# Block 1's inverse roots: one GpSimd power in place of a logarithm, an exponential and a correcting step, with new beats

## The reference, cut to what matters

```python
def _layernorm(x, axis=-1, eps=1e-05):
    m = jnp.mean(x, axis=axis, keepdims=True)
    v = jnp.var(x, axis=axis, keepdims=True)
    return (x - m) / jnp.sqrt(v + eps)
...
q = l2norm(q); k = l2norm(k)          # 16 heads of 64, each token's head by itself
dots = einsum('bhid,bhjd->bhij', q, k) * 10
dots = einsum('hg,bgij->bhij', W_pre_th, dots)      # "premix"
# causal mask; all but the 64 largest of a row are dropped; softmax
attn = einsum('hg,bgij->bhij', W_post_th, attn)     # "mix back"
out = einsum('bhij,bhjd->bhid', attn, v) * scale, times sigmoid(gates), @ Wo
x = _layernorm(x + out)
x = _layernorm(x + ffn(x))            # silu gate, two hidden layers with gelu
```

## Time and profile before

| | us |
|---|---|
| median of 3 runs | 3859.69 |
| lowest and highest run | 3850.48, 3867.26 |
| profiled execution | 3863.54 |
| its span (first to last instruction) | 3862.2 |
| TensorE busy | 3518.2 |
| VectorE busy | 3405.6 |
| ScalarE busy | 3078.7 |
| GpSimd busy | 1751.2 |
| granted TensorE clock, mean | 0.961 of full speed |

### The profile page before, as it was taken

How to read it: one execution, slowest core, us unless ns; L and a number is a source line. 1 busy time by engine, 2 the same in 40 slices (tenths; PEclk the granted TensorE clock), 3 DMA queues, 4 the chain that set the end, 5 groups by cost and what they waited for, 6 DMA issues and landing times.

```text
span 3862.2 us, 78954 instructions
## 1 busy us (share of the span) xinstructions
PE 3518.2 (91%) x19551; PEld 2607.6 (68%) x19551; DVE 3405.6 (88%) x18541; ACT 3078.7 (80%) x10773; POOL 1751.2 (45%) x3672
## 2 busy tenths in 40 slices
PE   4999999996799999999999999999999999999987
PEld 3888888873566666666666666666666666666665
DVE  6888888853999999999999999999999999999994
ACT  5777777755788888888888888888888888888864
POOL 0000000002556556565656555656666665665553
PEclk7999999996899999999999999999999999999999
DMA  3000000001111111111111111111111111111110
GB/s 125 12 12 9 12 12 12 10 6 35 26 28 28 29 32 28 28 32 34 33 30 28 28 29 28 28 28 30 31 28 29 34 33 33 28 28 29 26 26 4
DMA packets 168124, 106.01 MB, mean 27 GB/s; under 512 B 78000, under 2 KB 165104, under 8 KB 166896
## 3 DMA queue, kind: packets, MB, share of 16 engines
q1 hardware_dynamic: 167664, 100.96, 12.2%
HBM read 20.70 MB, written 8.91 MB: 8 GB/s over the span
## 4 chain that ended last, share of the span: by engine, by line
PE 32%; DVE 25%; ACT 16%; SPq 10%; DMA 8%; issue 7%; POOL 2%; DVEq 0%; ACTq 0%; POOLq 0%
SPq L1264 9%; DVE W L1736 8%; DMA T<-SN 8%; PE bank L362 6%; DVE last L1757 6%; ACT SN L1529 5%; PE bank L1336 4%; PE bank L1321 3%; PE bank L1413 3%; ACT T L1516 3%; PE bank L330 3%; PE bank L194 3%; PE bank L1348 2%; DVE y L895 2%; ACT L1485 2%
## 5 line engine op out<-in xcount | busy, mean ns | idle before, releaser
L1736 DVE MATCH_REPLACE8 W<-last,W 128x130 f32<-128x130 f32 (+17 forms) x3456 | 889.9, 269 | 0.0
L1757 DVE MAX8 last<-W 128x8 f32<-128x130 f32 (+17 forms) x3456 | 780.0, 271 | 0.0
L1842 POOL TENSOR_SCALAR posts<-post,share 128x128 f32<-128x128 f32 x1024 | 368.2, 378 | 372.7 <-DVE share L1666 372.7
L1336 PE MATMUL bank<-T,pre 128*128 128x40 f32 (+15 forms) x1024 | 402.8, 477 | 107.3 <-DMA T<-SN 79.1
L885 DVE TENSOR_TENSOR_SCAN hs<-dA,dx 128x256 f32<-128x256 f32 x512 | 353.2, 690 | 133.9 <-issue 100.5
L1516 ACT ACTIVATE T<-T,peak 128x260 f32<-128x260 f32 (+15 forms) x1024 | 416.7, 435 | 30.1 <-POOL T L1893 28.2
L1529 ACT ACTIVATE SN<-bank,rq 128x260 f32<-128x260 f32 (+1 forms) x1024 | 361.1, 433 | 88.0 <-DMA T<-SN 43.8
L1893 POOL TENSOR_TENSOR T<-T,below 128x520 f32<-128x520 f32 (+12 forms) x416 | 360.6, 883 | 23.1 <-DVE below L1766 7.6
L1336 PEld LDWEIGHTS bank<-T,pre 128*128 128x128 f32 x1024 | 173.4, 199 | 278.1 <-ACT T L1537 119.1
L1348 PEld LDWEIGHTS bank<-posts,T 128*128 128x128 f32 (+7 forms) x2048 | 267.9, 185 | 110.3 <-issue 54.7
L1348 PE MATMUL bank<-posts,T 128*128 128x128 f32 (+7 forms) x2048 | 324.4, 298 | 18.7 <-POOL posts L1842 17.2
(11 more groups left out here) (244 smaller groups left out, 9611.2 us busy)
## 6 DMA issues: line engine op xcount, KB each, us to landing
T<-SN SPq DMA_DIRECT2D x32, 130.0 KB
x_in<-in_xT SPq DMA_DIRECT2D x32, 128.0 KB, 2.2
x_mid<-x_b SPq DMA_DIRECT2D x32, 128.0 KB, 1.7
xb<-x_mid SPq DMA_DIRECT2D x32, 128.0 KB, 2.1
out_y<-x_d SPq DMA_DIRECT2D x32, 128.0 KB, 3.4
T<-SN SPq DMA_DIRECT2D x32, 126.0 KB
T<-SN SPq DMA_DIRECT2D x32, 122.0 KB
T<-SN SPq DMA_DIRECT2D x32, 118.0 KB
```

The costliest lines, as they stand in the source:

```text
L1336: pe.matmul(MIX[:, 0:pair.shape[-1]], pre[:], pair, start=True, stop=True).then_inc(premixed, 1)
L1736: dve.match_replace(both[:, s, at:to], best[n], both[:, s, at:to], LOWEST).then_inc(ranked, 1)
L1757: dve.max(best[n], both[:, s, at:to]).then_inc(ranked, 1)
L1842: pool.tensor_scalar(posts[(4 * k + j) % NP][:], post[:], share[k % 2][:, j:j + 1], 1.0, ALU.mult, ALU.mult).then_inc(posts_made, 1)
```

## The change

In the attention phase's two norms, for q and for k, `Root` is gone. GpSimd raises the clipped sums, or the variance with its epsilon, to the power -0.5 in one `tensor_tensor` with `ALU.pow` against a tile `power` that holds -0.5. ScalarE keeps in the norms only the copy with the epsilon (`act_lift`). Its table set for exponentials is now the one without the logarithm, and the gates' tanh no longer asks for the set of silu. The mixer phase's norms and the memory keys keep `Root`. New waits guard the tiles that the power writes or reads. All beat tables of the attention phase are new, and the loops run over one period more. Parts of the diff that only rename or repeat are left out.

```diff
@@ -36,7 +36,7 @@
-EXP_LN, SILU, GELU = "natural_log_exp_and_others", "silu_and_others", "gelu_and_others"
+EXP_LN, EXP, SILU, GELU = "natural_log_exp_and_others", "exp_and_others", "silu_and_others", "gelu_and_others"
@@ -96,12 +96,12 @@
     def __init__(self, room, sems, name, banks, sh, after, tiles):
...
-        self.var, self.rs, self.t = (room.sb(f"{name}_{n}", [P, 2]) for n in ("var", "rs", "t"))
-        self.meanmat, self.ident, self.eps = sh.meanmat, sh.ident, sh.eps
+        self.var, self.rs = (room.sb(f"{name}_{n}", [P, 2]) for n in ("var", "rs"))
+        self.meanmat, self.ident, self.eps, self.power = sh.meanmat, sh.ident, sh.eps, sh.power
...
-        self.lifted, self.normed, self.root = after.lifted, after.normed, after.root
+        self.lifted, self.normed, self.rooted = after.lifted, after.normed, sems.sem(name + "_rooted")
@@ -115,20 +115,20 @@
-    def act_root(self, act, k):
+    def act_lift(self, act, k):
...
-        act.wait_ge(self.lifted, k + 1)
-        self.root.act_guess(act, k, self.var[:], self.rs[:], self.t[:])
...
     def pool_root(self, pool, k):
-        k += self.base
-        self.root.pool_step(pool, k, self.var[:], self.rs[:], self.t[:])
+        pool.wait_ge(self.lifted, self.base + k + 1)
+        if k:
+            pool.wait_ge(self.spread, k)
+        pool.tensor_tensor(self.rs[:], self.var[:], self.power[:, 0:2], ALU.pow).then_inc(self.rooted, 1)
...
     def pe_spread(self, pe, k):
...
-        pe.wait_ge(self.root.stepped, Root.STEPS * (k + 1))
+        pe.wait_ge(self.rooted, k + 1 - self.base)
@@ -409,10 +409,10 @@
-        self.q_sq, self.q_t, self.rq = (room.sb(n, [P, 2 * HEADS]) for n in ("q_sq", "q_t", "rq"))
-        self.k_sq, self.k_t, self.rk = (room.sbs(n, [P, HEADS], 2) for n in ("k_sq", "k_t", "rk"))
+        self.q_sq, self.rq = (room.sb(n, [P, 2 * HEADS]) for n in ("q_sq", "rq"))
+        self.k_sq, self.rk = (room.sbs(n, [P, HEADS], 2) for n in ("k_sq", "rk"))
         self.x_loaded = sems.sems("xb_loaded", NXB)
-        self.q_root, self.k_root = Root(sems, "q"), Root(sems, "k")
+        self.q_rooted, self.k_rooted = sems.sem("q_rooted"), sems.sem("k_rooted")
@@ -480,12 +480,8 @@
-    def k_guess(self, act, b, t):
-        act.wait_ge(self.k_clipped, 2 * b + t + 1)
-        self.k_root.act_guess(act, 2 * b + t, self.k_sq[t][:], self.rk[t][:], self.k_t[t][:])
-
     def k_scale(self, act, b, t):
-        act.wait_ge(self.k_root.stepped, Root.STEPS * (2 * b + t + 1))
+        act.wait_ge(self.k_rooted, 2 * b + t + 1)
@@ -512,16 +508,15 @@
-    def q_guess(self, act, b):
-        act.wait_ge(self.q_clipped, b + 1)
-        self.q_root.act_guess(act, b, self.q_sq[:], self.rq[:], self.q_t[:])
-
     def k_clip(self, pool, b, t):
...
-    def k_step(self, pool, b, t):
-        self.k_root.pool_step(pool, 2 * b + t, self.k_sq[t][:], self.rk[t][:], self.k_t[t][:])
+    def k_power(self, pool, b, t):
+        pool.wait_ge(self.k_clipped, 2 * b + t + 1)
+        if b:
+            pool.wait_ge(self.k_scaled, 4 * (b - 1) + 2 * t + 2)
+        pool.tensor_tensor(self.rk[t][:], self.k_sq[t][:], self.sh.power[:, 0:HEADS], ALU.pow).then_inc(self.k_rooted, 1)
@@ -535,17 +530,22 @@
     def first_scale(self, dve, t):
-        dve.wait_ge(self.k_root.stepped, Root.STEPS * (t + 1))
+        dve.wait_ge(self.k_rooted, t + 1)
...
-    def q_step(self, pool, b):
-        self.q_root.pool_step(pool, b, self.q_sq[:], self.rq[:], self.q_t[:])
+    def q_power(self, pool, b):
+        pool.wait_ge(self.q_clipped, b + 1)
+        if b:
+            pool.wait_ge(self.s_kept, S_ALL * b)
+        pool.tensor_tensor(self.rq[:], self.q_sq[:], self.sh.power[:], ALU.pow).then_inc(self.q_rooted, 1)
...
     def q_clip(self, dve, b):
...
+        if b:
+            dve.wait_ge(self.q_rooted, b)
@@ -563,6 +563,7 @@
+        self.power, self.power_set = room.sb("power", [P, 2 * HEADS]), room.sem("power_set")
@@ -837,13 +838,11 @@
-                front.k_guess(act, 0, 0)
...
-                front.k_guess(act, 0, 1)
@@ -1031,11 +1029,13 @@
+        pool.memset(sh.power[:], -0.5).then_inc(sh.power_set, 1)
         mk_root.pool_step(pool, 0, mkv[:, 1:2], mkv[:, 3:4], mkv[:, 2:3])
+        pool.wait_ge(sh.power_set, 1)
...
-            front.k_step(pool, 0, t)
-        front.q_step(pool, 0)
+            front.k_power(pool, 0, t)
+        front.q_power(pool, 0)
@@ -1055,7 +1055,7 @@
-    SLOT, PERIODS = 16, SEQS + 2
+    SLOT, PERIODS = 16, SEQS + 3
@@ -1163,68 +1163,66 @@
-    PE_K = (-7, -6, 3, 3)
-    PE_K_TURN = (1, 2, 11, 24)
-    PE_Q = (11, 20, 23, 33)
-    PE_Q_SUM = (26, 30, 35, 36)
-    PE_Q_TURN = 44
-    PE_ATTEND = (5, 8, 8, 18)
-    PE_GATES = (34, 37, 39, 40)
-    PE_MIX = (56, 71, 89, 96, 121, 125, 126, 129)
-    PE_OUT = 25
-    PE_VAR1 = 33
-    PE_SPREAD1 = 38
-    PE_W1 = 41
-    PE_W2 = 45
-    PE_H1 = (63, 67, 67, 69)
-    PE_H2 = (79, 80, 91, 93)
-    PE_SCORE0 = (55, 60, 63)
-    PE_W3 = 94
-    PE_SCORE1 = (89, 91, 93, 95, 96, 100, 105, 107)
-    PE_VAR2 = 98
-    PE_SPREAD2 = 109
-    PE_V = (123, 127, 128, 128)
-    PE_PREMIX = [[71, 83, 89, 93, 104, 105, 118, 123], [125, 125, 128, 131, 136, 148, 164, 197]]
-    ACT_K = (-33, -24, 17, 21)
-    ACT_K_TURN = (9, 27, 30, 38)
-    ACT_Q = (30, 42, 43, 43)
-    ACT_K_ROOT = (-16, 24)
-    ACT_Q_SUM = 48
-    ACT_Q_ROOT = 55
-    ACT_PEAK = (-8, 33, 38, 42, 70, 78, 92, 114)
-    ACT_WIDE = (34, 39, 56, 69, 70, 80, 98, 123)
-    ACT_NARROW = (37, 41, 59, 69, 73, 85, 102, 127)
-    ACT_MIX = (68, 70, 72, 94, 96, 110, 119, 142)
-    ACT_SQUARE1 = 42
-    ACT_ROOT1 = 44
-    ACT_GATES = (44, 44, 51, 51)
-    ACT_SILU = (51, 52)
-    ACT_SCORE0 = (56, 63, 65)
-    ACT_H1 = (67, 68)
-    ACT_H2 = (74, 77)
-    ACT_SCORE1 = (72, 74, 77, 84, 85, 89, 91, 93)
-    ACT_SQUARE2 = 82
-    ACT_ROOT2 = 88
-    ACT_V = (114, 130, 138, 141)
-    ACT_PREMIX = [[69, 70, 75, 84, 90, 92, 97, 103], [109, 115, 144, 149, 158, 165, 191, 196]]
-    DVE_SHARE = (65, 83, 85, 98, 114, 117, 124, 136)
-    POOL_GATES = (15, 15, 17, 20)
-    POOL_OPEN = (80, 83, 85, 125)
-    ACT_CTX = (26, 28, 29, 33)
-    DVE_END1 = 62
-    DVE_Q_CLIP = 67
-    DVE_GATED = (73, 73)
-    DVE_END2 = 120
-    POOL_TURN = (-65, -65, -65, 8, 27, 56, 73, 63)
-    POOL_SHARE = (36, 62, 62, 80, 95, 106, 107, 124)
-    POOL_DROP = (8, 18, 34, 54, 67, 82, 105, 111)
-    POOL_ROOT1 = 25
-    POOL_Q_ROOT = 44
-    POOL_ROOT2 = 83
-    POOL_PREMIX = [[79, 80, 87, 104, 107, 107, 108, 110], [110, 122, 134, 139, 162, 168, 184, 193]]
-    ACT_K_SCALE = (3, 28)
-    POOL_K_CLIP = (-21, 10)
-    POOL_K_ROOT = (-14, 12)
+    PE_K = (1, 6, 21, 22)
+    PE_K_TURN = (18, 29, 34, 39)
+    PE_Q = (34, 36, 38, 44)
+    PE_Q_SUM = (42, 44, 48, 50)
+    PE_Q_TURN = 51
+    PE_ATTEND = (30, 31, 33, 34)
+    PE_GATES = (45, 51, 56, 60)
+    PE_MIX = (65, 79, 94, 106, 133, 136, 139, 146)
+    PE_OUT = 39
+    PE_VAR1 = 45
+    PE_SPREAD1 = 52
+    PE_W1 = 58
+    PE_W2 = 64
+    PE_H1 = (67, 72, 76, 78)
+    PE_H2 = (80, 89, 91, 95)
+    PE_SCORE0 = (64, 65, 69)
+    PE_W3 = 102
+    PE_SCORE1 = (85, 94, 96, 102, 103, 109, 115, 122)
+    PE_VAR2 = 112
+    PE_SPREAD2 = 136
+    PE_V = (141, 142, 145, 145)
+    PE_PREMIX = [[83, 91, 94, 102, 117, 123, 126, 135], [137, 140, 144, 156, 160, 165, 172, 204]]
+    ACT_K = (-38, -26, 1, 2)
+    ACT_K_TURN = (-5, 6, 20, 21)
+    ACT_Q = (18, 21, 23, 23)
+    ACT_Q_SUM = 33
+    ACT_PEAK = (-15, 5, 23, 36, 50, 58, 86, 109)
+    ACT_WIDE = (20, 22, 37, 44, 52, 74, 87, 111)
+    ACT_NARROW = (21, 33, 40, 47, 53, 80, 93, 111)
+    ACT_MIX = (46, 52, 70, 85, 91, 97, 106, 126)
+    ACT_SQUARE1 = 22
+    ACT_LIFT1 = 24
+    ACT_GATES = (23, 34, 38, 39)
+    ACT_SILU = (37, 37)
+    ACT_SCORE0 = (41, 43, 43)
+    ACT_H1 = (47, 50)
+    ACT_H2 = (53, 71)
+    ACT_SCORE1 = (55, 70, 73, 74, 78, 80, 82, 84)
+    ACT_SQUARE2 = 74
+    ACT_LIFT2 = 86
+    ACT_V = (110, 112, 118, 125)
+    ACT_PREMIX = [[52, 66, 71, 75, 82, 84, 90, 94], [101, 106, 126, 132, 146, 149, 154, 176]]
+    DVE_SHARE = (56, 82, 85, 105, 108, 118, 124, 137)
+    POOL_GATES = (9, 9, 20, 22)
+    POOL_OPEN = (25, 49, 70, 125)
+    ACT_CTX = (3, 7, 18, 19)
+    DVE_END1 = 61
+    DVE_Q_CLIP = 66
+    DVE_GATED = (73, 74)
+    DVE_END2 = 127
+    POOL_TURN = (-63, -63, -63, -36, -20, 36, 64, 65)
+    POOL_SHARE = (31, 46, 51, 67, 70, 72, 110, 116)
+    POOL_DROP = (-1, 22, 28, 34, 62, 66, 71, 114)
+    POOL_ROOT1 = 26
+    POOL_Q_ROOT = 30
+    POOL_ROOT2 = 109
+    POOL_PREMIX = [[65, 67, 67, 70, 72, 79, 101, 110], [111, 118, 118, 138, 156, 171, 192, 192]]
+    ACT_K_SCALE = (-6, 12)
+    POOL_K_CLIP = (-13, 3)
+    POOL_K_ROOT = (-13, 3)
@@ -1485,7 +1483,7 @@
-        table(EXP_LN)
+        table(EXP)
@@ -1519,7 +1517,7 @@
-                act.wait_ge(q_root.stepped, Root.STEPS * (b + 1))
+                act.wait_ge(q_rooted, b + 1)
@@ -1592,16 +1590,10 @@
-                    if b := whose(p, t, ACT_K_ROOT[n], 0):
-                        table(EXP_LN)
-                        front.k_guess(act, b, n)
```

(20 more changed lines are left out.)

3 lines of the change are left out of this document (removed).

## The result

| | median, us | lowest, highest |
|---|---|---|
| before, beside it | 3855.1 | 3848.2, 3867.3 |
| after | 4073.2 | 4061.6, 4080.3 |
| ratio | 1.0559 | 1.0521 to 1.0598 (95%) |

The changed kernel is 5.6% slower, some 218 us. The forecast was 3832, its range ended at 3905.

What follows compares the result with a forecast made beforehand. The prediction saw no single engine as bound but a loop through the engines' queues and the DMA. Seam terms of -25 us and tail -3 took 3863.5 to 3835.5, or 3832 in median terms; range 3750 to 3905.

Steps and rivals of the forecast that it cites:

- I take 0.3: GpSimd's power of 16 columns: 0.3 us, bounds 0.22 and 1.7, all covered, so no cost in a step.
- rival A: Power is slow: decides from 0.1 us a column, 3956 us at 0.2, 3882 at 0.15; chance 12%.
- The cover of q: Between q's turn and the first mix, TensorE's other pieces leave some 4 us to hide q's power.
- The cover of k: Between a key half's last square and its scaling, ScalarE's four copies less the clip leave 1.6 us.
- No VectorE work is removed: VectorE's work stays 84.5 us of an 89.3 us step.
- GpSimd is in it only by latency: The step is set by a loop through all engines' queues; GpSimd, busy 60%, matters only by its delay.
- The floor of 149 us: VectorE's work bounds a step, so any new order can give at most 31 x 4.8 = 149 us.
- The four terms of the seam: Between two sequences, per step: V's wait -1.15, bank's wait -0.7, DMA's wait +0.45, keys' scaling +0.6; sum -0.8 us.
- rival D: The seam clears: VectorE's wait of 2.9 us a step goes, and the low clock with it; 3767 us; chance 12%.
- The score phase: From first score block to last score, orders nearly alike: change taken as zero, bounds -1 and +1 us.
- The tail: Last sequence's two roots save 1.25 us each and a half-hidden table load 0.5; together -3 us.
- ScalarE's roots gone: Logarithms and exponentials leave ScalarE, 2.1 us a sequence; alone no gain, as it is busy 430 of 500 us.

Runs made afterwards that it cites:

- e1: The changed kernel with a product in place of each attention-block power (output not the reference's): 3779.9 us, ratio 0.9798.
- e5: The changed kernel with the power for q alone, products for k and the norms (output not the reference's): 4001.1 us, ratio 1.0376.
- e6: The changed kernel with the power for k alone, products for q and the norms (output not the reference's): 3858.2 us, ratio 1.0011.
- e7: The changed kernel with q's power two beats later, behind the first share's posts in GpSimd's list: 3958.5 us, ratio 1.0274.
- e8: As e7, with every power split into two halves of the columns, q's second half behind the second share: 3893.7 us, ratio 1.01.
- e17: As e16, with k's powers split into halves of 8 columns, q's whole: 3849.4 us, ratio 0.9966.
- e3: The changed code with the old beat tables and a product in place of the power (output not the reference's): 3888.7 us, ratio 1.009.
- e16: As e7, with VectorE's clip of q's sums five beats earlier in its list: 3889.7 us, ratio 1.0083.
- e12 to e15: Four runs: q's root or power moved behind the fourth drop in three kernels (3934.8, 3974.8, 4108.5 us); VectorE's q clip five beats earlier in e8 (3909.8 us).
- e18: As e16, with the first key half's clip and power ahead of the eighth drop in GpSimd's list: 4001.5 us, ratio 1.038.

## Why the prediction was wrong, point by point

- *"I take 0.3 ... At 0.3, and even at 1.7, all is covered, so the power costs nothing in a step."* This step failed. Both the value (2.93 us measured) and the upper bound were wrong. The bound came from the sequence that was replaced, which says what the change hopes to replace, not what an unseen operation can cost; and the value from the dearest simple row, though a power is not simple. e1, the same program with short roots, is 293 us faster. Nothing in the trace could have priced it, and the range should have said so.
- *The price of rival A.* Its decision point, 0.1 us a column, was right in kind: at 0.157 the kernel is slower. But its own formula would give 16 x 0.157 - 1.6 = 0.9 for k and 5.0 - 4 = 1.0 for q, 59 us, less 28: 3891, and with A's whole formula at 0.2 it was 3956. Measured is 4073. The cover was mis-sized too.
- *The cover of q, "some 4 us".* I counted TensorE's pieces between turn and mix as if GpSimd could start at the turn. It starts at the clip, which stands some 5 us later in VectorE's list. With a product (e1) the root starts at 2032.53 and the first score copy at 2035.55: 3.0 us. The power is 5.44 long, 2.4 over, and 2.39 is ScalarE's wait. The posts have less: 5.2 us later than with a product, TensorE waits 4.72 for them, so their cover was 0.5. q costs 7.1 us a sequence (e5), where 5.4 less the 4 of the prediction would be 1.4. The prediction had no term for the low clock behind such a wait.
- *The cover of k, 1.6 us.* Near: ScalarE waits for `rk` 61.0 us, 2.0 a sequence over both halves, 2.93 - 1.6 = 1.3 being the longest of one. k costs 2.5 a sequence (e6).
- *"No VectorE work is removed".* Right, but the work was taken as fixed, 84.5 us a step, and it grew: 83 us in all after, 67 with k's powers alone (e6 against e1). The change's effect on how long VectorE's own instructions take had no term.
- *The loop, "GpSimd is in it only by latency".* Right, and it is the reading that the experiments bear out: 115 us from one number (e7), a gain in spite of more GpSimd work (e8, e17). The floor of 149 us a new order could give was right as well: e1 is 2.0% under before, 71 us by the medians, and so inside it.
- *The four terms of the seam.* V's wait went, as said (35.8 to 9.1). The bank's wait did not (22.8 to 23.8; it is the premix's, L1336, not the first mix's as the prediction has it). The DMA's wait was to grow by 0.45 a sequence and fell a little (72.4 to 67.0; e1 66.3). The keys' scaling came late by 1.1 (e1, 32.5 us in 30), against my 0.6 of 0 to 1.6. In e1 these sum to about +0.1, and yet e1 gains 2.5 a sequence: that came from VectorE, whose seam wait fell from 89.8 to 65.6 and whose wait for row sums from 56.7 to 6.1. The prediction names the second wait and gives it no term. That is the mechanism of rival D in part, and the low clock went with it in part: 72 us at 0.50 from 1000 to 3700 us in e1, 140 before, and TensorE's same 19551 matmuls take 3474.1 us where they took 3518.2.
- *The score phase, taken as zero.* e1 does not contradict it. With the power, this is where q's loss is (the stops for `posts` and `rq`), which the bounds of -1 and +1 did not hold.
- *Table loads.* 189, as counted.
- *The tail.* The first root's power ran 0.73 us where root and steps took 1.57. 0.84 gained where 1.25 was forecast, in the right place, and nothing beside 218.
- *ScalarE's roots gone, "alone no gain".* Right, and on the far side: e3, without that work and without GpSimd's steps, loses 0.9%.

## What to carry to other kernels

An operation that no row shows has no upper bound from its neighbours or from what it replaces; where the decision hangs on it, give its slow case the weight of ignorance, or measure it first. A cover runs from when the input is truly made, on the engine that makes it, so read where the last producer stands in its own list, not only where data could be ready. In a loop of fixed lists a long instruction costs what is queued behind it; move the waited-for piece ahead, cut the instruction, or bring its input earlier, and test each, since four such steps here gave 115, 65, 69 and 40 us (e7, e8, e16, e17), and five more gave nothing or cost up to 150 (e12 to e15, e18). A long wait of TensorE is dearer than its length where the granted clock falls behind it. And an engine's work is not fixed by its instruction count: compare its busy time between runs before the rest of a price is put down to waits.
